# Output projection and later queries of a graph attention layer in f16 parts, with the first query job four steps later

## The reference

```python
h = jnp.maximum(_layernorm(x, axis=-1), 0.0)          # sources
hs = layer_norm(h, ln1_scale, ln1_bias)               # 2048 x 256, eight heads of 32
ht = layer_norm(h_target, ln1_scale, ln1_bias)
q = (ht @ Wq + bq).reshape(T, H, HD) / jnp.sqrt(jnp.float32(HD))
k = (hs @ Wk + bk).reshape(S, H, HD)
v = (hs @ Wv + bv).reshape(S, H, HD)
logits = jnp.where(edge_mask[None] != 0, jnp.einsum('thd,shd->hts', q, k), NEG)
ctx = jnp.einsum('hts,shd->thd', jax.nn.softmax(logits, axis=-1), v).reshape(T, D)
ht = ht + ctx @ Wo + bo
ht = layer_norm(ht, ln2_scale, ln2_bias)
return x + ht + jax.nn.gelu(ht @ W1) @ W2             # W1: 256 x 1024, W2: 1024 x 256
```

## Time and profile before

| | us |
|---|---|
| median of 3 runs | 690.22 (690.02 to 692.46) |
| the profiled execution | 694.41 |
| its span | 692.6 |
| PE busy | 657.6 (95%) |
| DVE busy | 569.2 (82%) |
| POOL busy | 524.2 (76%) |
| ACT busy | 484.0 (70%) |
| first context product | 72 |
| end of the last unit | 593.5 |

### The profile page before, as it was taken

The page is one execution under the profiler, slowest core; times in us unless marked ns, Lnnn a source line. Parts: engine busy times, 40 slices in busy tenths (PEclk is TensorE's granted clock), DMA queues, the critical chain, the costliest instruction groups (busy, mean ns, idle before and its releaser), DMA issues. The chain is left out here.

```text
span 692.6 us, 20346 instructions
## 1 busy us (share of the span) xinstructions
PE 657.6 (95%) x8346; PEld 473.0 (68%) x8346; DVE 569.2 (82%) x946; ACT 484.0 (70%) x932; POOL 524.2 (76%) x488
## 2 busy tenths in 40 slices
PE   4898999999999999999999999999999899899998
PEld 4465667766776777677767766777777567557767
DVE  5987899989999879999997798989868888575661
ACT  4865668766778858677787686778866788867550
POOL 3574889889999957899998678999977777471430
PEclk9998999999999999999999999999999999999999
DMA  8735501113001011220011112012000000000001
GB/s 296 258 80 153 177 31 36 59 63 108 2 2 34 2 62 63 58 82 2 2 33 33 62 33 78 17 51 74 2 2 2 2 3 2 1 1 32 24 17 54
DMA packets 20797, 36.23 MB, mean 52 GB/s; under 512 B 2752, under 2 KB 13280, under 8 KB 20704
## 3 DMA queue, kind: packets, MB, share of 16 engines
q1 hardware_dynamic: 20704, 34.92, 16.2%
HBM read 26.49 MB, written 2.10 MB: 41 GB/s over the span
## 5 line engine op out<-in xcount | busy, mean ns | idle before, releaser
L1412 POOL TENSOR_TENSOR prob_lo<-prob 128x512 f16<-128x512 f32 x382 | 437.1, 1169 | 74.1 <-ACT prob L888 73.2
L888 ACT ACTIVATE prob<-score 128x512 f32<-128x512 f32 x512 | 304.1, 597 | 135.8 <-PE score L469 128.3
L469 PE MATMUL score<-nidentb,mask_nat 128*128 128x128 bf16 x2048 | 199.1, 220 | 4.1 <-ACT qT L905 1.9
L469 PE MATMUL early<-kT,qT 96*128 96x512 f16 x512 | 192.9, 382 | 10.5 <-DVE half_max L1203 10.1
L469 PEld LDWEIGHTS ctx<-v_sb,prob 128*128 128x128 bf16 x2048 | 159.0, 98 | 60.2 <-ACT raw L910 12.6
L469 PE MATMUL score<-qT,kT 97*128 97x512 f16 x512 | 196.3, 383 | 0.0
L1203 DVE CUSTOM_DVE_ANT_0 early<-early,mask_nat,half_max 128x1024 f32<-128x1024 f32 x128 | 163.6, 1287 | 38.0 <-PE early L469 36.0
L469 PE MATMUL ctx<-v_sb,prob 128*128 128x65 f16 x2048 | 191.4, 193 | 2.3 <-ACT raw L910 1.8
L469 PE MATMUL ctx<-v_sb,prob_lo 128*128 128x65 f16 x2048 | 190.4, 193 | 0.0
L469 PEld LDWEIGHTS ctx<-v_sb,prob_lo 128*128 128x128 f16 x2048 | 142.6, 97 | 49.9 <-issue 4.0
L1203 DVE CUSTOM_DVE_ANT_0 early<-early,mask_nat 128x1024 f32<-128x1024 f32 x128 | 157.1, 1229 | 22.5 <-PE early L469 20.8
(11 more groups left out here) (167 smaller groups left out, 623.2 us busy)
## 6 DMA issues: line engine op xcount, KB each, us to landing
adj_in<-in_adj SPq DMA_DIRECT2D x26, 512.0 KB, 4.0
qT<-q_stage SPq DMA_DIRECT2D x48, 64.0 KB, 2.0
kT<-mask_nat SPq DMA_DIRECT2D x48, 64.0 KB, 2.0
raw<-in_x SPq DMA_DIRECT2D x4, 512.0 KB, 5.6
tgt<-in_L_gnn_h_target SPq DMA_DIRECT2D x4, 512.0 KB, 11.6
prob<-in_adj SPq DMA_DIRECT2D x4, 512.0 KB, 10.4
nT<-in_L_gnn_W SPq DMA_DIRECT2D x2, 1024.0 KB, 6.6
mask_nat<-in_x SPq DMA_DIRECT2D x1, 2048.0 KB, 8.3
```

Source lines behind the costliest of these rows:

```text
L469: return nc.tensor.matmul(dst, w, m, start=start, stop=stop, **more)
L888: nc.scalar.activation(prob[:, n % SLOTS, :], score[n % 2][:, :], ACT.Exp).then_inc(exp_done, 1)
L1412: nc.gpsimd.tensor_tensor(prob_lo[:, n % SLOTS, :], prob[:, n % SLOTS, :], prob_hi(n % SLOTS), ALU.subtract).then_inc(lo_sem["pool"], 1)
```

## The change

Output rows and the queries of blocks 1 to 3 become f16 products: each f32 operand is split into a high f16 part and the f16 rest, and three of the four part products are made. Targets' features are stored as a quarter, in parts (t_parts), with an identity of fours (quad16) to read them back, and query weights as four times theirs. For this ACT makes a high part and DVE a low part of the features (feature_high, feature_low) and of the context (context_T, context_low), ACT and POOL split Wo in unit 2, ACT and DVE split Wq in unit 3. context_low now is the last reader of a context transpose. The first query job moves from (4, 1) to (4, 5), two masks from (4, 7), (5, 3) to (5, 1), (5, 4) and one from (4, 3) to (4, 5). In the start, source group 1 is dropped before group 2 is normed, 24 products that nobody reads stand after values(0), values come later and early scores sooner, and the statistics and the square root of target blocks 1 and 2 move behind the start into units 0 and 1.

```diff
-QP_AT = {(4, 1): 0, (4, 11): 1}
+QP_AT = {(4, 5): 0, (4, 11): 1}
-MASK_DVE = [(1, 0), (2, 3), (2, 6), (3, 2), (3, 7), (4, 3), (4, 7), (5, 3)]
+MASK_DVE = [(1, 0), (2, 3), (2, 6), (3, 2), (3, 7), (4, 5), (5, 1), (5, 4)]
...
+T_HIGH = {0: [(1, 1), (1, 2)], 1: [(3, 8), (3, 14)]}
+T_LOW = {0: [(1, 2), (1, 3)], 1: [(4, 0), (4, 1)]}
+WO_UNIT, WQ_UNIT = 2, 3
...
+                    if t == 0:
+                        pe.wait_ge(wo_lo, 1)
+                        pe.wait_ge(t_lo, DC * (k + 1))
                     dst = aux[:, t % 2 * D:(t % 2 + 1) * D]
+                    part = slice(t * P, (t + 1) * P)
                     for c in range(DC):
-                        mm(dst, cT[:, c, t * P:(t + 1) * P], wo[:, c, :], c == 0, False, skip_group_check=True)
+                        for a, w in ((0, 0), (0, 1), (1, 0)):
+                            mm(dst, c_parts[:, a, c, part], wo_parts[:, w, c, :], c == a == w == 0, False, skip_group_check=True)
                     for c in range(DC):
-                        last = mm(dst[:, c * P:(c + 1) * P], nTq[:, k % 2, c, t * P:(t + 1) * P], ident32[:, :], False,
-                                  c == DC - 1, skip_group_check=True)
+                        for a in range(2):
+                            last = mm(dst[:, c * P:(c + 1) * P], t_parts[k % 2][:, a, c, part], quad16[:, :], False,
+                                      c == DC - 1 and a == 1, skip_group_check=True)
...
                 def queries(k, m, c):
                     if c == 0:
                         aux_free(("qp", k, m))
-                    last = mm(aux[:, :], wq[:, c, m * P:(m + 1) * P], nTq[:, k % 2, c, :], c == 0, c == DC - 1)
+                        pe.wait_ge(t_lo, DC * (k + 1))
+                        pe.wait_ge(wq_lo, 1)
+                    for i, (w, a) in enumerate(((0, 0), (1, 0), (0, 1))):
+                        last = mm(aux[:, :], wq_parts[:, w, c, m * P:(m + 1) * P], t_parts[k % 2][:, a, c, :], c == i == 0,
+                                  c == DC - 1 and i == 2)
...
-                    nc.scalar.activation(cT[:, c, :], aux[:, :], ACT.Copy).then_inc(aux_done, 1)
+                    nc.scalar.activation(c_parts[:, 0, c, :], aux[:, :], ACT.Copy).then_inc(c_hi, 1)
...
+                        if u == 1 and s == 3:
+                            for b in (1, 2):
+                                target_deviation(b)
...
+                def feature_low(k, c):
+                    dve.wait_ge(t_hi, DC * k + c + 1)
+                    parts = t_parts[k % 2]
+                    nc.vector.scalar_tensor_tensor(out=parts[:, 1, c, :], in0=t_full[k][:, c, :], scalar=QUARTER, in1=parts[:, 0, c, :],
+                                                   op0=ALU.mult, op1=ALU.subtract).then_inc(t_lo, 1)
...
+                def context_low(k, c):
+                    dve.wait_ge(c_hi, DC * k + c + 1)
+                    nc.vector.tensor_tensor(c_parts[:, 1, c, :], aux[:, :], c_parts[:, 0, c, :], ALU.subtract).then_inc(aux_done, 1)
...
+                            if k > 0 and (r, s - 1) in CT_AT:
+                                context_low(k - 1, CT_AT[r, s - 1])
...
+                        if u == 0 and j == 3:
+                            target_stats(2)
-                        if u == 0 and j in (4, 5):
+                        if u == 1 and j in (4, 5):
                             target_norm(j - 3)
...
                     if f == 5:
                         block_low(1)
+                    if f in (6, 7):
+                        context_low(NTB - 1, f - 6)
...
                 source_norm(1)
+                drop_sources(1)
                 source_norm(2)
-                drop_sources(1)
```

More of the change, by code:

```diff
@@ L608, in shift_row @@
                     for t in range(TT):
[L609 removed]
+                        last = mm(aux[0:SHIFT_ROW + 1, t * P:(t + 1) * P], shift[:, t, :], quad16[:, :], True, True)
                     last.then_inc(aux_ready, 1)
@@ L690, in _ @@
                 values(0)
+                for i in range(UNREAD_LATER):
+                    mm(early[1][:, TB:TB + P], identb[:, :], identb[:, :], True, True)
+                project(2)
                 turn_rows(3)
-                project(2)
                 values(1)
@@ L1010, in _ @@
                 high_parts(3)
-                for k in range(1, 3):
-                    target_deviation(k)
                 nc.scalar.activation(warm_c, eps_c, ACT.Exp).then_inc(act_link, 1)
+                high_parts(4)
                 high_values(2)
-                high_parts(4)
                 feature_sum(0)
```

135 lines of the change are left out of this document (92 added, 43 removed).

## The result

| | us |
|---|---|
| the changed kernel, median of 6 runs | 708.11 (707.25 to 713.09) |
| the kernel before, median of 6 runs beside it | 691.34 (689.96 to 694.53) |
| ratio, 95% interval | 1.0242 (1.0206 to 1.0278) |
| the profiled execution, its span | 710.03, 708.2 |

A forecast was written before the change was run, and what follows sets the result against it. PE bounds the kernel, DVE next by 1 to 2 us in some units. Terms +5.8 (r = 4, 5), -0.9 (r = 2, 3), +1.2 (units 0 to 3), -2.6 (start), 0 (tail) sum to +3.5: 693.7 from median 690.2, range 687.5 to 698.5.

The forecast's parts named there:

- PE work taken away: f16 products save PE 2.5 us in units 4, 12, 20, 5.2 in six output-row units and 1.7 in the tail.
- Waits added, r = 4: Units 4, 12, 20: shift row waits for query_low 4.2 us, waits for t_lo with lead_scale 5.4, lost cover 3.4.
- The wait for t_lo: At s = 5 queries wait for DVE's feature_low: 1.8 us in unit 4, 1.2 each in units 12 and 20.
- Rival C: More than forecast: port contention stretches feature_low to 1.5 us (+4.8) or half clock falls on project(3); 697 to 700, chance 0.1.
- the forecast 1.7: Units 12 and 20: without query steps to cover ACT's two table loads at s = 1, PE loses 1.7 us each.
- The gain at s = 10: Units 12 and 20: the stalls give DVE time, so PE's wait on DVE at s = 10 goes, 2.0 us.
- The mask moved out of the start of r = 5: Units 5, 13, 21 lose the 0.9 us by which they are longer than unit 6, 2.7 in all.
- The start: Earlier project(2) and first scores at 61.6 against 64.82 gain 2.6 us, bounds 1 and 5.
- Units 0 to 3: target_deviation with two table loads in unit 1 costs 0.7 us, feature_low and parts about 0.5: +1.2, bounds 0 and 3.5.
- Units 10, 18, 26: context_low on DVE delays second transposes, shift row and scores: 0.95 us each in units 18 and 26, 2.35 in unit 10.
- The tail: Four output rows save 1.7 us, but context_low(0) delays transposes and next products 1.7: net 0, bounds -1.7 and +1.
- all cases: Own case 691.5 to 696, chance 0.5; the others 681 (0.1), 689 to 691 (0.3), 697 to 700 (0.1).

The follow-up runs named there:

- e2: The changed kernel with its last two mask halves back at (4,7) and (5,3): 705.19 us, ratio 1.0182.
- e14: The kernel before with only the last three mask halves moved, to (4,5), (5,1), (5,4): 694.52 us, ratio 1.0023.
- e8: The changed kernel with the tail's first context_low ahead of block_low(1) on DVE: 706.82 us, ratio 1.0212.
- e13: The kernel before with the whole new start alone, statistics and square root of target blocks 1 and 2 in units 0 and 1: 693.70 us, ratio 1.0027.
- e7: The changed kernel with statistics and square root of target blocks 1 and 2 back in the start: 709.30 us, ratio 1.0246.
- e12: The kernel before with some low parts of the exponential moved from DVE to POOL in units 4, 10, 12, 18, 20, 26: 690.07 us, ratio 0.9969.

## Why the prediction was wrong, by its own steps

**PE work taken away: right.** The six units with output rows and the three with queries have the work that was forecast: unit 11 went from 18.92 to 18.05 (-0.87, forecast 0.86), and a step with half a query job from 1.76 to 1.55 (four such steps a unit: 0.84). The forecast 9.4 us of PE's work are gone, and what was added takes back all of it and 15.3 more.

**Waits added, r = 4: right in kind, 1.2 us low.** The shift row waits 1.32 us in each of the three units (forecast 1.4). The wait for t_lo is 1.29 in unit 12 (1.2), the same in unit 20 at full clock, and 2.98 in unit 4 (1.8). The missing 1.2 in unit 4 are the first feature_low at 1.32 us, not 0.7, and the prob_lo behind it at 1.52. The 0.6 by which lead_scale was to lengthen the shift wait of units 12 and 20 did not come: it is 1.32 there as in unit 4. Of six feature_low three took 1.32 us and three 0.68, one of each per unit. In unit 4 POOL works without a break from 137.82 to 143.19, the slow one lies beside that, and the one that starts at 143.42, with POOL idle, takes 0.68. Rival C had this cause at up to 4.8 us; three times 0.64 are 1.9. The row that it stood on (prob_lo 678 to 1555) was the better guess for an operation with both operands in SBUF next to a busy POOL. By the Trainium skill (SBUF — State Buffer, SBUF: two separate sides) that is the shared port pair, and the trace agrees: 1.32 for the three beside POOL, 0.68 for the three without. By the distances between steps PE loses 2.1 us around the table loads in unit 12, where it lost 0.4: the forecast 1.7. The gain at s = 10 came, 1.0 in each of units 12 and 20.

**The mask moved out of the start of r = 5: the largest error, 4.9 us.** The step said that the move "removes the 0.9 us by which units 5, 13 and 21 are longer than unit 6". It followed the mask that leaves the head of the unit, (4,7), and not where it lands, (5,1). The wait at the head did go (0.49 us before 159.34 in the profile before). But 0.23 at s = 10 and 1.23 at s = 14 came for it. There are two masks within unit 5 both before and after, since DVE reaches (4,7) when PE is 1.5 us into unit 5. What changed is where they lie beside POOL and DVE's other work (POOL's row last). Before:

```profile
155.89 0.69 DVE L1191 TENSOR_SCALAR mask_nat<-adj_in 128x1024 bf16<-128x1024 int32 x1
163.78 1.38 DVE L1191 TENSOR_SCALAR mask_nat<-adj_in 128x1024 bf16<-128x1024 int32 x1
155.95 4.97 POOL L1412 TENSOR_TENSOR prob_lo<-prob 128x512 f16<-128x512 f32 x4 [0.61 <-ACT prob L888]
```

And after:

```profile
165.60 1.47 DVE L1271 TENSOR_SCALAR mask_nat<-adj_in 128x1024 bf16<-128x1024 int32 x1
171.75 1.31 DVE L1271 TENSOR_SCALAR mask_nat<-adj_in 128x1024 bf16<-128x1024 int32 x1
162.00 8.40 POOL L1503 TENSOR_TENSOR prob_lo<-prob 128x512 f16<-128x512 f32 x7 [0.72 <-ACT prob L919]
```

The first mask used to start 0.06 us ahead of a run of POOL and took 0.69; now it starts in the middle of one and takes 1.47. The two together take 2.78 us for 2.07, and unit 6 shows that DVE has only 1.2 us to spare in a unit of 14.9. The second stands right ahead of a low part of 1.52 us, and behind both PE waits at s = 14. e2 and e14 each show the effect alone, 0.75 a unit: e2 with the old places in the changed kernel, e14 with the new ones in the kernel before. So the expectation of e2, that two masks instead of one make these units long, had the right places and the wrong reason.

**The start: 3.3 us, and no gain at all.** The -2.6 were the half clock of project(2) in one trace (3.65 us for four records) and of the way to the first context product (0.51 in the earlier trace rows). At full clock the old start ends at 67.7 and the new at 68.3 to 68.7 in eight traces (69.6 in one, e8). The first scores, forecast at 61.6 against 64.82, are at 62.9, and with the old start at full clock at 62.6. The work that the new order does sooner in one place it waits for in another: in the changed kernel PE waits 1.52 us before project(3) and 1.02 before the shift row.

```profile
38.64 1.96 PE L487 MATMUL ctx<-nT,cT 128*128 128x512 f32 x4 [1.52 <-issue]
...
61.75 0.43 PE L487 MATMUL aux<-quad,shift 128*97 128x128 f16 x4 [1.02 <-ACT shift L931]
```

There was an error of method in it too. The prediction scaled from the profiled 694.4 down to the median of 690.2, and the difference of 4.2 is that same half clock; then it took most of it off once more as the start's gain.

**Units 0 to 3: 1.9 us low.** e13 shows 2.1 for the new start and the work that it moved there (forecast 0.7); the rest came with the f16 parts (feature_low and the weight parts), which no run takes out alone. "PE already waits there on DVE, under which most of it lies" was wrong for the table loads: at s = 6 of unit 1 PE waits 2.32 us for them, where it waited 1.39 for DVE, and DVE is late after that (0.18 more at s = 14). e7 shows that taking them out again uncovers DVE.

**Units 10, 18, 26: the second context_low at a third of its price.** Unit 18 loses the forecast 0.6 before the second transposes (by distances between steps; the row's idle time is 0.41). For the second context_low 0.35 was forecast, and PE loses 0.2 at the shift row and 0.7 at s = 10, where it waits 0.56 for maxima. Net +0.6 where 0.1 was forecast, the same in unit 26. Unit 10 waits 1.41 and 0.56, +1.6 against a forecast of 1.5.

**The tail: right at full clock.** PE waits 2.41 us for context_low(0), 1.6 more than before, and the four rows give it back: 99.1 against 99.15. In the profile after, half clock behind the wait adds 1.7:

```profile
623.20 0.63 PE L642 MATMUL aux<-ident,q_stage 128*128 128x128 f32 x4 [2.41 <-DVE cT L1264]
623.66 5.74 PE L487 MATMUL score<-qT,w_f 128*128 128x512 f16 x18
```

**The range** ended at 698.5, since all cases were built on the same start and the same r = 5. The two steps that failed, the mask's move (-2.7 forecast, +2.2 measured) and the start's gain (-2.6 forecast, +0.7 measured), erred with one sign and left the bounds that the steps themselves had given.

## What to carry to other kernels

Where a second engine is within one or two us of the bound in a stretch, work taken from the first is worth what stands ahead of the next wait, and an operation added to the second engine ahead of something that the first waits for can cost as much as was saved (here 0.69 us of context_low eight times for 6.9 us of products). For a thing that is moved, follow it to where it lands, and take its length from rows at that place: the same mask took 0.69 us at one place and 1.47 at another. Before a gain is read from a slow row, see whether it was slow in every execution: a mean clock beside each time tells that, and one trace doesn't.

## What the runs showed of the hardware

Executions of the same kernel fall on a few levels of the mean granted clock, and time goes with it: from 689.9 us at 1.000 to 697.0 at 0.988, about a microsecond for each 0.0017. A wait of PE of 0.9 to 3 us is followed by a stretch at the lower level (1.2 GHz) in one execution and not in another: 2.98 us in unit 4 with half clock from 144.2 in the changed kernel, and without in e2; 1.19 us before project(2) with it in the earlier trace rows, and without in e12.

What an operation of DVE costs beside POOL goes by whether POOL is at work when it starts. A feature_low of 128x512 in SBUF takes 0.68 us with POOL idle and 1.32 beside it. In the profile before, ahead of the tail, all 12 masks that start while POOL is idle take 0.68 to 0.69 us, also where POOL begins right behind, and the 14 that start while POOL runs take 0.71 to 2.32. Of the low parts of DVE 35 start while POOL is idle and take 0.68 to 0.69; 95 start while it runs, and 78 of these take longer, up to 1.55. query_low and context_low, with one operand in PSUM, take 0.66 to 0.75 in the changed kernel's trace, although POOL runs when they start (all but two in the tail).

A table load is 1.28 us, and ACT's next operation starts within 0.02 us behind it.
